# A routed first stage: choosing experts by maxima, counting earlier, and moving the last shared products behind the first rows

## The reference, cut to what matters

```python
xn = _layernorm(x, axis=-1)
x = x + _L0_attn_ref(xn, ...) + _L0_ffn_ref(xn, ...)
# _L0_ffn_ref: 8 experts, 4 groups of 2, the best 2 groups, of their experts the best 2
scores = jax.nn.sigmoid(logits)
sfc = scores + bias[None, :]
group_scores = jnp.sum(jax.lax.top_k(grp, 2)[0], axis=-1)
grp_idx = jax.lax.top_k(group_scores, TOPK_G)[1]
masked = jnp.where(score_mask > 0, sfc, 0.0)
topk_idx = jax.lax.top_k(masked, TOP_K)[1]
topk_w = jnp.take_along_axis(scores, topk_idx, axis=1)
topk_w = topk_w / (jnp.sum(topk_w, axis=-1, keepdims=True) + 1e-20)
# plus one shared expert (352 wide) for every token
out = routed.reshape(orig_shape) + _mlp(x, shared_gate_w, shared_up_w, shared_down_w)
```

## Time and profile before

| what | us |
|---|---|
| median of 3 runs | 1756.43 |
| the runs | 1755.75 to 1758.14 |
| profiled execution | 1741.03 |
| its span | 1739.2 |

### The profile page before, as it was taken

One profiled execution on the slowest core, in us unless ns is written; L12 is line 12 of the kernel. 1 busy time (PEld: TensorE's weight loads), 2 busy tenths in 40 slices (PEclk: granted clock), 3 DMA queues, 4 the chain that ended last, 5 costly groups with the idle time before them and its releaser, 6 DMA issues.

```text
span 1739.2 us, 41709 instructions
## 1 busy us (share of the span) xinstructions
PE 1663.8 (96%) x14092; PEld 1226.2 (71%) x14092; DVE 1466.3 (84%) x3682; ACT 1203.6 (69%) x2912; POOL 1101.9 (63%) x1149
## 2 busy tenths in 40 slices
PE   8999899999999999999999999999987689999989
PEld 5577567777777777777777777777765566777677
DVE  6322599999999999999999999999996699999963
ACT  3034477777777777777777777777763488888863
POOL 1700067777777777776666666666666578888851
PEclk9999999999999999999999999999998699999999
DMA  9433310111110101100101000001002000000023
GB/s 316 165 107 105 98 32 23 38 32 27 31 36 21 40 21 37 30 24 25 27 15 30 15 27 24 18 24 27 15 9 61 1 1 2 1 2 2 1 77 107
DMA packets 66098, 73.85 MB, mean 42 GB/s; under 512 B 10975, under 2 KB 54767, under 8 KB 65775
## 3 DMA queue, kind: packets, MB, share of 16 engines
q1 hardware_dynamic: 62919, 63.92, 12.7%
q0 software_dynamic: 3072, 8.65, 1.5%
HBM read 55.45 MB, written 17.10 MB: 42 GB/s over the span
## 4 chain that ended last, share of the span: by engine, by line
PE 81%; DVE 8%; ACT 4%; POOL 3%; issue 2%; DMA 1%; SPq 0%; DVEq 0%; POOLq 0%
PE banks L781 20%; PE banks L940 7%; PE banks L808 4%; PE banks L895 3%; PE banks L816 3%; PE banks L914 3%; PE banks L824 3%; PE banks L746 3%; PE banks L853 3%; PE banks L861 3%; PE banks L867 2%; PE banks L1075 2%; PE banks L860 2%; PE banks L996 2%; PE banks L765 2%
## 5 line engine op out<-in xcount | busy, mean ns | idle before, releaser
L781 PE MATMUL banks<-xnT,hw 128*128 128x512 f32 x768 | 414.4, 623 | 2.5 <-DVE cv L2094 2.5
L2150 DVE CAST_PREDICATED MM<-lmask,banks 128x512 bf16<-128x512 uint32 x384 | 272.8, 710 | 38.6 <-PE banks L861 34.5
L2094 DVE SCALAR_TENSOR_TENSOR cv<-banks,hc,cv 128x510 f32<-128x510 f32 (+2 forms) x384 | 285.2, 743 | 5.5 <-ACT cv L1495 0.8
L1559 ACT ACTIVATE T<-banks 128x256 bf16<-128x256 f32 x384 | 149.3, 389 | 154.8 <-PE banks L853 153.7
L2761 POOL TENSOR_TENSOR X<-X,yrow 128x512 f32<-128x512 f32 x128 | 163.2, 1276 | 68.0 <-ACT yrow L1591 68.0
L2725 POOL TENSOR_TENSOR kn<-nsum,half_pos 128x4 f32<-128x4 f32 x64 | 65.5, 1023 | 143.4 <-DVE nsum L2119 143.4
L861 PEld LDWEIGHTS banks<-MM,T 128*128 128x128 bf16 x1536 | 103.9, 98 | 64.3 <-issue 47.4
L860 PEld LDWEIGHTS banks<-T,MM 128*128 128x128 bf16 x1280 | 98.8, 97 | 66.3 <-ACT T L1559 64.7
L2094 DVE SCALAR_TENSOR_TENSOR cv<-banks,hcv,cv 128x510 f32<-128x510 f32 (+2 forms) x192 | 141.5, 737 | 1.4 <-ACT cv L1495 1.3
L853 PEld LDWEIGHTS banks<-MM,Gb 128*128 128x128 bf16 x1536 | 83.9, 98 | 82.8 <-issue 43.0
L940 PE MATMUL banks<-ho,OT 128*128 128x256 f32 x512 | 142.2, 401 | 0.0
(11 more groups left out here) (319 smaller groups left out, 4833.0 us busy)
## 6 DMA issues: line engine op xcount, KB each, us to landing
MM<-in_eye SPq DMA_DIRECT2D x64, 256.0 KB, 2.7
slot_rows<-zeros SPq DMA_DIRECT2D x1, 5304.0 KB, 20.9
xs<-slot_rows SPq DMA_DIRECT2D x13, 408.0 KB, 3.9
slot_out<-ye SPq DMA_DIRECT2D x13, 384.0 KB, 2.7
hw<-in_hw SPq DMA_DIRECT2D x16, 256.0 KB, 3.5
wT<-in_winit SPq DMA_DIRECT2D x8, 384.0 KB, 4.3
wgu<-in_wgu SPq DMA_DIRECT2D x1, 2816.0 KB
w1c<-in_ew SPq DMA_DIRECT2D x16, 176.0 KB
```

What stands on the lines that cost most here:

```text
L781: ins = pe.matmul(PROJ[t][:], hw[:, kk, t, :], xnT[:, kk, u.b * BLK:(u.b + 1) * BLK], start=(kk == 0), stop=(kk == KD - 1))
L1559: act.activation(strips(T1[:].rearrange("p i t -> p (i t)"), LEVELS[lv], 0, 1), grams_bank(u)[:, 0:TILES * 64].rearrange("p (k e) -> p k e ...
L2094: dve.scalar_tensor_tensor(o, y, taps_of(t)[:, TAPS - 1 - i:TAPS - i], o, ALU.mult, ALU.add).then_inc(dve_conv, 1)
L2150: dve.copy_predicated(dst, m, ps).then_inc(dve_mm, 1)
```

## The change

Five things change, all in the first stage.

1. The choice of experts. The 8 by 8 comparison (four operations of 1024 elements) is gone. Instead `largest` finds the greatest of a token's eight values, marks those that reach it, turns the marks into places, takes the smallest place and marks it alone; the value is then lowered by 3e38 and the second is found in the same way. Step 7 does the group's mask and the product in one operation. The weights take one operation fewer (the scale 2.5 goes into the division's product).
2. The last logits stand ahead of the first half product of piece 1, and the count's four matmuls stand among the fourth pair of products instead of behind it.
3. `slots` is written in two halves. POOL starts after the first, and waits for the second ahead of the second sends.
4. After the third block's down products PE multiplies zeros seven times.
5. The fourth block's 12 down matmuls no longer stand ahead of the expert tiles. Six stand behind the first tile's transposes and six behind the second's.

```diff
-MASK_STEPS = 13
-ROUTING_STEPS = MASK_STEPS + 6 + 4 + 9 + 4
+MASK_STEPS = 19
+ROUTING_STEPS = MASK_STEPS + 5 + 4 + 9 + 4
...
             logits(2)
             pe.wait_ge(ln_kept0, NBLK + 2)
             pe.wait_ge(ln_kept1, NBLK + 2)
-            shared_gate(1, 0)
             pe.wait_ge(s_const, 10 * 16)
             logits(3)
-            shared_gate(1, 1)
+            for kk in range(KD):
+                shared_gate(1, kk)
...
-            shared_down(NBLK - 1)
-
+
+            pe.wait_ge(m_h, FS0 * NBLK)
+            for _ in range(7):
+                pe.matmul(bank[5][:, 0:2 * P], zeros[:, 0:P], zeros[:, 0:2 * P], start=True, stop=True)
             pe.wait_ge(e_ids, 1)
             pe.wait_ge(e_w, 2 * 16)
...
                 if n < TILES0:
                     turn_x(n)
+                    if n < 2:
+                        shared_down(NBLK - 1, range(n * TPB // 2, (n + 1) * TPB // 2))
...
-            ranks(r_gs[:], 4, lt4)
-            step(dve.tensor_scalar(r_gs[:], r_rank[:, :, 0:4], 2.0, None, ALU.is_lt))
-            step(dve.tensor_tensor(r_mask[:].rearrange("p t (g e) -> p t g e", e=2), pairs,
-                                   r_gs[:].unsqueeze(3).to_broadcast([P, NT, 4, 2]), ALU.mult))
-            ranks(r_mask[:], 8, lt8)
-
-            step(dve.tensor_scalar(r_mask[:], r_rank[:], 2.0, None, ALU.is_lt))
+            ranks(r_gs[:], r_gs[:], 4, lt4)
+            each_group = [v[:].rearrange("p t (g e) -> p (t g) e", e=2) for v in (r_mask, r_sfc)]
+            ranks_twice = r_gs[:].rearrange("p t g -> p (t g)").unsqueeze(2).to_broadcast([P, NT * 4, 2])
+            step(dve.scalar_tensor_tensor(each_group[0], ranks_twice, 2.0, each_group[1], ALU.is_lt, ALU.mult))
...
+            def largest(v, chosen):
+                step(dve.tensor_reduce(top, v, AX.X, ALU.max))
+                step(dve.tensor_tensor(found, v, top.unsqueeze(2).to_broadcast([P, NT, E0]), ALU.is_ge))
+                step(dve.scalar_tensor_tensor(found, places, float(NT * P), found, ALU.subtract, ALU.mult))
+                step(dve.tensor_reduce(top, found, AX.X, ALU.min))
+                step(dve.tensor_tensor(chosen, found, top.unsqueeze(2).to_broadcast([P, NT, E0]), ALU.is_equal))
+
+            largest(r_mask[:], chosen_of[0])
+            step(dve.scalar_tensor_tensor(r_rank[:], chosen_of[0], -3e38, r_mask[:], ALU.mult, ALU.add))
+            largest(r_rank[:], chosen_of[1])
+            step(dve.tensor_tensor(r_mask[:], chosen_of[0], chosen_of[1], ALU.add))
...
-            step(dve.tensor_tensor(r_w[:], r_w[:], r_den[:].unsqueeze(2).to_broadcast([P, NT, E0]), ALU.mult))
-            step(dve.tensor_scalar(r_w[:], r_w[:], SCALE0, None, ALU.mult))
+            step(dve.scalar_tensor_tensor(r_w[:], r_w[:], SCALE0, r_den[:].unsqueeze(2).to_broadcast([P, NT, E0]), ALU.mult, ALU.mult))
...
-            dve.tensor_copy(slots[:], slotf[:]).then_inc(e_slots, 1)
+                dve.tensor_copy(slots[:, :, k], slotf[:, :, k]).then_inc(e_slots, 1)
...
                 pool.wait_ge(e_ids, 1)
+                pool.wait_ge(e_slots, TOP0)
```

More of the change, by code:

```diff
@@ L687, in _ @@
                 shared_raise(2, kk)
-            for kk in range(KD):
-                shared_gate(3, kk)
+            chosen = r_mask[:].rearrange("p t e -> p (t e)")
+            shared_gate(3, 0)
+            pe.wait_ge(rt, MASK_STEPS)
+            pe.matmul(bank[6][:, 0:1], chosen, ones_col, start=True, stop=True).then_inc(pe_once, 1)
+            shared_gate(3, 1)
+            pe.wait_ge(*s_spread)
+            pe.matmul(bank[6][:, P:2 * P], tri, chosen, start=True, stop=False)
+            pe.matmul(bank[6][:, P:2 * P], counts[:], cross, start=False, stop=True)
+            pe.matmul(bank[6][:, 2 * P:2 * P + E0], counts[:], per_e, start=True, stop=True).then_inc(pe_once, 1)
             for kk in range(KD):
@@ L698, in shared_up, with shared_down @@
                         shared_raise(n, kk)
-            def shared_down(b):
+            def shared_down(b, those=range(TPB)):
                 pe.wait_ge(m_h, FS0 * (b + 1))
@@ L703, in shared_down @@
                     pe.wait_ge(e_slots, 1)
-                for t in range(TPB):
+                for t in those:
                     if b and t % 2 == 0:
@@ L711, in shared_down @@
                         last.then_inc(m_down, 1)
[L713 to L720, removed]
             shared_up(1)
@@ L1993, in over, with ranks @@
                 return (v.unsqueeze(2) if axis == 0 else v.unsqueeze(3)).to_broadcast(shape)
-            def ranks(v, n, lt):
+            def ranks(rank, v, n, lt):
                 gt = r_gt[:, :, 0:n * n].rearrange("p t (i j) -> p t i j", i=n)
@@ L2000, in ranks @@
                 step(dve.copy_predicated(gt, lt[:].bitcast(U32).unsqueeze(1).to_broadcast([P, NT, n, n]), eq))
-                step(dve.tensor_reduce(r_rank[:, :, 0:n], gt, AX.X, ALU.add))
+                step(dve.tensor_reduce(rank, gt, AX.X, ALU.add))
             s8 = sig0[:, :, NH:NH + E0]
@@ L2006, in _ @@
             step(dve.tensor_tensor(r_gs[:], pairs[:, :, :, 0], pairs[:, :, :, 1], ALU.add))
-            ranks(r_gs[:], 4, lt4)
-            step(dve.tensor_scalar(r_gs[:], r_rank[:, :, 0:4], 2.0, None, ALU.is_lt))
-            step(dve.tensor_tensor(r_mask[:].rearrange("p t (g e) -> p t g e", e=2), pairs,
-                                   r_gs[:].unsqueeze(3).to_broadcast([P, NT, 4, 2]), ALU.mult))
-            ranks(r_mask[:], 8, lt8)
-            step(dve.tensor_scalar(r_mask[:], r_rank[:], 2.0, None, ALU.is_lt))
+            ranks(r_gs[:], r_gs[:], 4, lt4)
+            each_group = [v[:].rearrange("p t (g e) -> p (t g) e", e=2) for v in (r_mask, r_sfc)]
+            ranks_twice = r_gs[:].rearrange("p t g -> p (t g)").unsqueeze(2).to_broadcast([P, NT * 4, 2])
+            step(dve.scalar_tensor_tensor(each_group[0], ranks_twice, 2.0, each_group[1], ALU.is_lt, ALU.mult))
+            places = edges[:, 0:E0].unsqueeze(1).to_broadcast([P, NT, E0])
+            found, top = r_eq[:, :, 0:E0], r_den[:]
+            chosen_of = [r_gt[:, :, k * E0:(k + 1) * E0] for k in range(TOP0)]
+            of_rank = r_gt[:, :, TOP0 * E0:(TOP0 + 1) * E0]
+            def largest(v, chosen):
[8 more added lines that the diff above has]
+            step(dve.tensor_tensor(r_mask[:], chosen_of[0], chosen_of[1], ALU.add))
             assert steps == MASK_STEPS
-            step(dve.scalar_tensor_tensor(r_w[:], r_rank[:], 2.0, s8, ALU.is_lt, ALU.mult))
+            step(dve.tensor_tensor(r_w[:], r_mask[:], s8, ALU.mult))
             step(dve.tensor_reduce(r_den[:], r_w[:], AX.X, ALU.add))
@@ L2018, in _ @@
             step(dve.reciprocal(r_den[:], r_den[:]))
-            step(dve.tensor_tensor(r_w[:], r_w[:], r_den[:].unsqueeze(2).to_broadcast([P, NT, E0]), ALU.mult))
-            step(dve.tensor_scalar(r_w[:], r_w[:], SCALE0, None, ALU.mult))
-            of_rank = r_gt[:, :, 0:E0]
+            step(dve.scalar_tensor_tensor(r_w[:], r_w[:], SCALE0, r_den[:].unsqueeze(2).to_broadcast([P, NT, E0]), ALU.mult, ALU.mult))
             def weights_of(k):
-                step(dve.scalar_tensor_tensor(of_rank, r_rank[:], float(k), r_w[:], ALU.is_equal, ALU.mult))
+                step(dve.tensor_tensor(of_rank, chosen_of[k], r_w[:], ALU.mult))
                 step(dve.tensor_reduce(w1st[:] if k else xnr[:, :, D], of_rank, AX.X, ALU.add))
@@ L2040, in _ @@
             for k in range(TOP0):
-                step(dve.scalar_tensor_tensor(of_rank, r_rank[:], float(k), r_slot[:], ALU.is_equal, ALU.mult))
+                step(dve.tensor_tensor(of_rank, chosen_of[k], r_slot[:], ALU.mult))
                 step(dve.tensor_reduce(slotf[:, :, k], of_rank, AX.X, ALU.add))
-            dve.tensor_copy(slots[:], slotf[:]).then_inc(e_slots, 1)
+                dve.tensor_copy(slots[:, :, k], slotf[:, :, k]).then_inc(e_slots, 1)
             weights_of(1)
```

## The result

| kernel | median us | runs | lowest to highest |
|---|---|---|---|
| before | 1755.74 | 20 | 1753.23 to 1758.14 |
| changed | 1759.16 | 20 | 1755.80 to 1764.75 |

The ratio is 1.0021, with a 95% interval of 1.0014 to 1.0027: 3.4 us slower, where +0.3 was forecast, and inside the range. The profile of before had taken 1741.03 us, 15 less than its own timed runs; that of the changed kernel took 1758.84, like its timed runs. So the two profiles can't be subtracted: of the +17.8 us between the spans, the timed runs show only 3.4.

The account below looks back on a forecast made before the run. Two paths, the sorted rows and PE's shared products, reach the first tile 0.73 us apart; PE is gapless behind it. Rows -3.6 and moved products +3.9 give +0.3: 1756.43 to 1756.7 us, range 1753.6 to 1760.0.

Parts of the forecast that it names:

- Mask, weights, slots: 1.8 + 0.26 + 0.65 us: DVE's routing: gains from 13 small mask steps (4.2 us), one weight step fewer, and POOL released a product-and-sum pair earlier.
- Rows 3.6 us earlier: Routing to PE: shorter logits, mask, weights and slots bring the sorted rows to PE at 87.85 instead of 91.45.
- thin cover: PE's count matmuls end near 38.1, some 0.6 us before DVE asks; each 0.1 later takes 0.1 off the gain.
- the logits' 0.9: Last logits, no longer behind the half product, end 0.95 us earlier; ACT's idle time limits the gain to 0.9.
- The late count: Rival at DVE's wait for the count: a wait of 1 us gives +1.3, 1757.7 us; chance 0.06.
- First up product 0.3 later than 93.16, wrong after 95: Start of the experts on PE: about 0.3 us later; forecast wrong if before 92 or after 95.
- Zeros hidden, PE waits 1.35 us: PE before the rows: 3.1 us of zeros end at 86.5, then PE waits 1.35 us until 87.85.
- The wait here is about as long, so it should stay: PE's wait for the rows: clock stays at 1.00; rival of a fall costs 1.7 us more, 1758.4, chance 0.10.
- One cast more while the first send runs: DVE beside POOL's first send: the extra cast would take 0.18 us or less off the gain; left out.
- The move costs 3.9 us behind the rows: First tiles on PE: 5.2 us of moved down products, less 1.27 of waiting that they fill.
- 2.8 us faster if the move were left out: Down products left in place: PE through at 88.6, 0.75 behind the rows, kernel 2.8 us faster.
- The sum, +0.3: First up product and end of experts: rows 3.6 us earlier, move costs 3.9, so +0.3; forecast chance 0.72.

Follow-up runs that it names:

- no zeros: The changed kernel without its seven products of zeros; 1741.95 us, ratio 1.0009 to the kernel before on the same chip.
- before again: The kernel before, rerun without an edit; 1741.38 us against 1740.86, ratio 1.0002.
- changed again: The changed kernel, rerun without an edit; 1741.64 us against 1741.19 for the kernel before, ratio 1.0000.
- logits back: The changed kernel with one half product again ahead of the last logits; 1741.17 us, ratio 1.0003 to the kernel before.
- downs back: The changed kernel without zeros, the fourth block's twelve down matmuls again ahead of the wait for the rows; 1738.07 us, ratio 0.9982 to before.
- the delayed kernels: Before and changed kernels, each with 46 more products of zeros ahead of the tiles; 1757.62 and 1757.08 us, ratios 1.0095 and 1.0098 to before undelayed.

## Why the prediction was right, and where it was not

- *Mask, weights, slots: 1.8 + 0.26 + 0.65 us.* Right. 13 steps in 4.22 us; the new operations cost what a sum and a product of the same size cost.
- *Rows 3.6 us earlier.* Right where PE keeps its clock (first send 3.5 earlier in no zeros, from the same start), wrong in both profiles of the changed kernel: 1.6 earlier than before in the first (43.9 against 45.5), 0.3 in the second (44.8 against 45.1). The step that failed is the count's "thin cover" of 0.6 us, and in part the logits' 0.9. I took PE's clock as given because PE was never idle there, and it fell to half in or behind narrow products in a row. DVE then waited 1.18 and 2.26 us for the count. Of the logits' 0.9, a late start of PE, no work of the change, took 0.7 in the first; in the second the start took 0.2 and the slow clock 0.6. The late count was one of my rivals, but with no cause and a chance of 0.06; it came in both profiles.
- *First up product 0.3 later than 93.16, wrong after 95.* Wrong by that sign in both profiles of the changed kernel: 113.90 with the stretch, 96.17 without. Less the late start (0.2), the second is 3.2 behind before again: 4.0 for the move, and 0.7 instead of 3.6 won on the rows.
- *Zeros hidden, PE waits 1.35 us.* Hidden in changed again and in logits back, with 1.12 and 1.91 us of waiting. In changed again the size is luck: the zeros began 2.8 us later than worked out (86.20 against 83.4) and the rows came 2.7 later (90.50 against 87.85), because the same fall of the clock held back both.
- *"The wait here is about as long, so it should stay"*, of the clock. Wrong in one of two: behind 1.91 us of waiting in logits back the clock was at 0.50 from 90.2 to 93.6 us, at a price of 1.5 us (1.7 worked out); behind 1.12 us in changed again it stayed.
- *One cast more while the first send runs.* It did not: the second cast ran from 43.55 to 43.73, and the first send began at 43.93, 1.11 us behind the first cast's start, as before.
- *The move costs 3.9 us behind the rows.* Right, and measured alone at 3.98 in the profile.
- *2.8 us faster if the move were left out.* Right in time: downs back, 2.8 under before; with the logits' order back too, 3.6.
- *The range.* It is the forecast with 3.1 us down and 3.3 up; the doubts named for it, 1, 1.7 and 2, would add up to 4.7 upwards. The result lies inside either.
- *The sum, +0.3.* Where PE was fed normally, the ratio is 1.0000 with 1.6 us either way, so in time the trade is about even within that. The mechanism behind it is not the forecast's in the one profile that exists there, which has +3.2 at the first up product. In the first measurement it was +3.4, from 2.5 to 4.7, and the other 3 us are not explained. That session had 14.5 us more on before and 17.5 more on the changed kernel. That before had the stretch too, and that it is 3 us worse for the changed kernel, is only argued: no profile of before in that state exists, and a delay of PE of the same size by other means gave no such difference. One candidate was not tested: where PE is the path, what the fall behind the logits takes from it is paid in full. It took 1.7 us in the first profile and 3.4 in changed again, and on top of the 0.2 that the delayed kernels differ by from the same start that would be 1.9 to 3.6, an estimate. What starts the stretch is open.

## What to carry to other kernels

When two paths meet at one wait with less than a microsecond between them, an earlier arrival of one is worth no more than that difference; take the gain by making both shorter, and do not move work of the full engine behind the meeting point, except as much as fits its idle gap there (here 1.27 us, six instructions of 24), and even that pays only if this engine is the later of the two. Ask of PE's order not only whether it is idle: a long row of narrow products can cost it the clock as a wait can, in some executions and not in others, and a step with thin cover behind it then pays. And compare a profile's own time with the timed runs, and the start of the stage in both, before subtracting profiles; here the first differed by 15 us, the second by up to 1.5.

## What the hardware showed that I had not expected

- The clock at 0.50 for about 3 to 7 us while PE was fully busy by the profile, in or behind 32 logits instructions of 24 columns, in 4 of 6 profiles with that order and 0 of 8 without it. It took 1.7 to 3.4 us from PE.
- A stretch of 14 us (74 to 88) in which PE was given six matmul instructions with no wait shown, while POOL's sends kept their 0.96 us each.
- The kernel before at 1741 us on three chips and at 1756 in the timed runs of the first measurement, whose range was 4.9 us.
